# A gated cross-attention and mixture-of-experts layer: attention stacked through DRAM, tokens sorted by expert

## What is computed

```python
x = x + tanh(g_xattn[0]) * xattn(layernorm(x), ctx, ctx, wq, wk, wv)
x = x + tanh(g_ffn[0]) * ffn(layernorm(x), Wr, br, W1, b1, W2, b2)
# xattn: Q, K, V by 16 heads of 8; softmax(Q K^T / sqrt(8)) V
# ffn: D = 128, hidden 256, E = 8, K = 2
logits = jnp.einsum('btd,de->bte', x, Wr) + br
topv, topi = jax.lax.top_k(logits, K)
sel_mask = jax.nn.one_hot(topi, E, dtype=logits.dtype).sum(-2) > 0
gates = jax.nn.softmax(jnp.where(sel_mask, logits, neg_inf), axis=-1)
h = jax.nn.relu(jnp.einsum('btd,edh->bteh', x, W1) + b1)
out = jnp.einsum('bte,bteh,ehd->btd', gates, h, W2)
out = out + jnp.einsum('bte,ed->btd', gates, b2)
```

## Time and profile before

| | us |
|---|---|
| median of 3 runs (816.5 to 819.39) | 818.69 |
| the profiled execution | 816.67 |
| its span, from the first instruction to the last | 814.7 |
| TensorE busy | 731.7 |
| VectorE busy | 586.8 |
| ScalarE busy | 561.7 |
| GpSimd busy | 357.9 |

### The profile page before, as it was taken

The page is one execution under the profiler, slowest core; times in us unless marked ns, Lnnn a source line. Parts: engine busy times, 40 slices in busy tenths (PEclk is TensorE's granted clock), DMA queues, the critical chain, the costliest instruction groups (busy, mean ns, idle before and its releaser), DMA issues. The chain is left out here.

```text
span 814.7 us, 24508 instructions
## 1 busy us (share of the span) xinstructions
PE 731.7 (90%) x7494; PEld 592.9 (73%) x7616; DVE 586.8 (72%) x2271; ACT 561.7 (69%) x1301; POOL 357.9 (44%) x524
## 2 busy tenths in 40 slices
PE   3678999989899998999989999898979999999997
PEld 1455787878678786778868787777867878787765
DVE  3777878777777777777767777577777777778643
ACT  3587777767667675867767687576767767677532
POOL 4555444544444443454444344344444445444400
PEclk9867999999999999999999999799999999999999
DMA  5000000000000000010000001000000000000000
GB/s 174 2 1 23 1 23 14 23 15 22 17 3 23 14 23 16 2 36 2 23 16 23 15 2 36 2 23 15 22 16 2 23 14 23 15 2 15 1 15 13
DMA packets 20583, 15.20 MB, mean 19 GB/s; under 512 B 1552, under 2 KB 20112, under 8 KB 20208
## 3 DMA queue, kind: packets, MB, share of 16 engines
q1 hardware_dynamic: 19632, 13.21, 5.4%
q10 hardware_dynamic: 832, 0.41, 0.2%
HBM read 9.42 MB, written 4.19 MB: 17 GB/s over the span
## 5 line engine op out<-in xcount | busy, mean ns | idle before, releaser
L962 POOL TENSOR_TENSOR probs_lo<-probs 77x512 bf16<-77x512 f32 x256 | 261.5, 1041 | 137.8 <-ACT probs L533 137.6
L449 PE MATMUL y<-w_sb,hidden 128*128 128x128 f32 x2048 | 286.3, 285 | 0.0
L449 PEld LDWEIGHTS y<-w_sb,hidden 128*128 128x128 f32 x2048 | 268.3, 198 | 3.9
L560 ACT ACTIVATE hidden<-hidden_p,b_sb 128x512 f32<-128x512 f32 x256 | 175.5, 686 | 70.2 <-PE hidden_p L431 70.1
L533 ACT ACTIVATE probs<-scores 77x512 f32<-77x512 f32 x256 | 152.2, 595 | 8.3 <-PE scores L373 7.9
L708 DVE TENSOR_REDUCE neg_max<-max_scores 128x4 f32<-128x308 f32 x256 | 120.7, 471 | 34.8 <-PE max_scores L355 34.3
L724 DVE SCALAR_TENSOR_TENSOR acc<-y,gates,acc 128x128 f32<-128x128 f32 x384 | 107.9, 344 | 35.9 <-PE y L449 35.9
L428 PE MATMUL hidden_p<-xT,w_lo 128*128 128x512 bf16 x253 | 100.1, 396 | 20.2 <-issue 12.2
L373 PE MATMUL scores<-qmT,kT 128*77 128x128 bf16 x1024 | 103.8, 226 | 1.8 <-ACT probs L533 1.7
L373 PEld LDWEIGHTS scores<-qmT,kT 128*77 128x77 bf16 x1024 | 85.7, 121 | 26.8 <-issue 5.7
L431 PE MATMUL hidden_p<-xT_mid,w_sb 128*128 128x512 bf16 x256 | 98.7, 385 | 0.6 <-ACT xT_mid L656 0.4
(11 more groups left out here) (102 smaller groups left out, 1178.5 us busy)
## 6 DMA issues: line engine op xcount, KB each, us to landing
x_in<-x SPq DMA_DIRECT2D x16, 256.0 KB, 3.1
out<-result SPq DMA_DIRECT2D x16, 256.0 KB, 2.3
ctx_in<-ctx_t SPq DMA_DIRECT2D x16, 154.0 KB, 3.0
w_sb<-w SPq DMA_DIRECT2D x2, 1024.0 KB, 12.5
b_rows<-b ACTq DMA_DIRECT2D x1, 384.0 KB, 9.9
w_att<-w_att_t SPq DMA_DIRECT2D x1, 192.0 KB, 5.1
gates_in<-g_xattn ACTq DMA_DIRECT2D x1, 0.5 KB, 3.3
gates_in<-g_ffn ACTq DMA_DIRECT2D x1, 0.5 KB, 4.9
```

Source lines behind the costliest of these rows:

```text
L449: last = mm(y_bank[:, cut], hidden[k][:, cut], w2_sb[:, w], start=False, stop=(c == HC - 1), skip_group_check=True)
L560: nc.scalar.activation(hidden[m % 4][:], hidden_bank[m % 2][:], ACT.Relu, bias=b1_sb[:, m:m + 1]).then_inc(s_relu, 1)
L962: G.tensor_tensor(probs_lo[h][:], probs[h][:], upper(probs[h][:]), ALU.subtract).then_inc(s_plo[h], 1)
```

## The change

It is a rewrite. The sequences 0 to 55 are sorted by expert in five chunks of 8, 12, 12, 12 and 12; the sequences 56 to 63 go through all experts as before. The program is a list of 100 slots without loops; a planner at build time gives the slots of routing, scattering, experts, gathering and adding. By its rules the quads stand in slots 37, 39 to 43, 51 to 58, 63 to 70 and 75 to 90, the scattered rows in slots 30 to 33, 42 to 47, 54 to 59, 66 to 71 and 78 to 80, the gathers of the last chunk in 93 to 95, the experts of the last eight sequences in 81 to 96.

Attention: projections are made per four sequences (512 or 308 columns). K and Q, split in high and low bf16 halves, are stored to DRAM and read back so that a head's 8 rows lie interleaved as (high, high, low, ones or maxima) on 32 partitions; the maxima take the same way. The transposes of Q and K on TensorE go. The products with V keep the f32 probabilities and write head j's 9 rows to the strip of 32 partitions j of one bank; ScalarE copies that bank, TensorE turns it with four f32 transposes, VectorE normalises. The probabilities' low halves are no longer made.

Experts: for each chunk VectorE ranks the tokens by expert, and GpSimd scatters each token's row twice to DRAM, to its place among its experts' rows. The rows are read back in quads of four tiles of 128, turned by the transfer itself; 38 quads in all. Each tile belongs to one expert, whose number TensorE loads from SBUF into a register (`name_weights`), and the weights' addresses are made from it. ScalarE stores the outputs from its own queue; GpSimd gathers each token's two outputs; VectorE adds both with their gates. Biases of the hidden layer become a product (`b1_split`). Weights, the cleared rows and constants are moved in pieces from ScalarE's queue.

```diff
-ATT_LAG = 2
-EXPERT_LAG = 7
+CHUNKS = (8, 12, 12, 12, 12)
+DENSE = 8
+MAX_LAG = 8
+SCORE_LAG = 13
+OUT_LAG = 14
+ROUTER_LAG = 20
...
+QUADS = [(2 * n + 8) // 4 for n in CHUNKS]
+ROUTED = [SEQ0[c] + CHUNKS[c] - NB + ROUTER_LAG for c in range(NC)]
+RANKED = [t + 2 for t in ROUTED]
+PLACED = [t + 5 for t in ROUTED]
+SCATTER_AT, QUAD_AT, ADD_AT = [], [], []
+t = 0
+while len(ADD_AT) < SB:
+    late = t >= LAST_ATT
+    for _ in range(4 if late else 2):
+        last = QUAD0[CHUNK_OF[len(ADD_AT)]] + QUADS[CHUNK_OF[len(ADD_AT)]] - 1 if len(ADD_AT) < SB else NQ
+        if len(SCATTER_AT) < SB and PLACED[CHUNK_OF[len(SCATTER_AT)]] < t:
+            SCATTER_AT.append(t)
+        elif len(QUAD_AT) > last and QUAD_AT[last] + 3 <= t:
+            ADD_AT.append(t)
+    if len(QUAD_AT) < NQ and t not in RANKED:
+        c = CHUNK_OF_QUAD[len(QUAD_AT)]
+        whole = SEQ0[c] + CHUNKS[c]
+        if len(SCATTER_AT) >= whole and SCATTER_AT[whole - 1] + (2 if late else 4) <= t:
+            QUAD_AT.append(t)
+    t += 1
+GATED_ALL = B - NB + ROUTER_LAG
+DENSE_AT = [GATED_ALL + 1 + n for n in range(DENSE // NB * E)]
...
-        head = h * PER + j
-        o = o_bank[:, head * VW:(head + 1) * VW]
-        v = v_cols[n % 4][:, head, :]
-        mm(o, hi[:, j * S:(j + 1) * S], v, start=(head == 0), stop=False,
-           skip_group_check=True)
-        last = mm(o, probs_lo[h][:, j * S:(j + 1) * S], v, start=False, stop=True,
-                  skip_group_check=True)
-    last.then_inc(p_pv, 1)
+def values(b, h):
...
+    pe.wait_ge(s_exp, HG * b + h + 1)
+    for j in range(PER):
+        last = mm(oT_bank[ROWS * j:ROWS * j + VW, h * S:(h + 1) * S], v_cols[g % 3][:, b % NB, h * PER + j, :],
+                  probs[h][:, j * S:(j + 1) * S], start=True, stop=True, skip_group_check=True)
+    last.then_inc(p_pv, 1)
+def turn_o(b, t):
+    pe.wait_ge(s_oT, b + 1)
...
+    for h in range(HG):
+        last = nc.tensor.transpose(o_bank[:, h * S:(h + 1) * S], oT[:, h * S:(h + 1) * S], ident[:])
+    last.then_inc(p_oT, 1)
...
+def name_weights(q):
...
+    _, held[q] = nc.values_load_multi_w_load_instructions(
+        tile_w[c % 2][0:1, at_tile:at_tile + 4], engines=[mybir.EngineType.PE], min_val=0,
+        max_val=(E - 1) * HID, skip_runtime_bounds_check_because="DVE clamps the expert's number to 0..7")
+def hidden_part(q, half):
+    k = 2 * q + half
+    if half == 0:
+        pe.wait_ge(s_xs[q % 3], 32 * (q // 3 + 1))
...
+    if k:
+        pe.wait_ge(s_relu, k)
+    w_hi, tiles = upper(w1_sb[:]), xsT[q % 3]
+    for t in range(2 * half, 2 * half + 2):
+        w = held[q][t]
+        cut = slice(t * 128, (t + 1) * 128)
+        for m in range(HC):
+            o = hidden_bank[:, ((t % 2) * HC + m) * 128:((t % 2) * HC + m + 1) * 128]
+            at_w = bass.ds(w + m * 128, 128)
+            mm(o, b1_split[:, at_w], ones_b[:], start=True, stop=False, skip_group_check=True)
+            mm(o, w_hi[:, at_w], tiles[:, 0, cut], start=False, stop=False, skip_group_check=True)
+            mm(o, w1_lo[:, at_w], tiles[:, 0, cut], start=False, stop=False, skip_group_check=True)
+            last = mm(o, w_hi[:, at_w], tiles[:, 1, cut], start=False, stop=True, skip_group_check=True)
+    last.then_inc(p_hid, 1)
+def rows_out(q):
+    pe.wait_ge(s_relu, 2 * q + 2)
...
+    for t in range(4):
+        w = held[q][t]
+        o = y_bank[:, t * 128:(t + 1) * 128]
+        mm(o, ones_b[:], b2_split[:, bass.ds(w, 128)], start=True, stop=False, skip_group_check=True)
+        for m in range(HC):
+            last = mm(o, hidden[:, (2 * q + t // 2) % 4, t % 2, m, :], w2_sb[:, bass.ds(w + m * 128, 128)],
+                      start=False, stop=(m == HC - 1), skip_group_check=True)
+    last.then_inc(p_y, 1)
+def dense_units(n):
...
+    w_hi = upper(w1_sb[:])
+    for m in range(HC):
+        cut = slice(e * HID + m * 128, e * HID + (m + 1) * 128)
+        mm(score_bank[m][:], w_hi[:, cut], dense_rows[g % 2][:, 0, :], start=True, stop=False,
+           skip_group_check=True)
+        mm(score_bank[m][:], w1_lo[:, cut], dense_rows[g % 2][:, 0, :], start=False, stop=False,
+           skip_group_check=True)
+        mm(score_bank[m][:], w_hi[:, cut], dense_rows[g % 2][:, 1, :], start=False, stop=True,
+           skip_group_check=True).then_inc(p_dhid, 1)
+def dense_out(n):
...
+    for i in range(NB):
+        o = to[:, i * D:(i + 1) * D]
+        mm(o, ones_b[:], b2_split[:, e * HID:e * HID + D], start=True, stop=False, skip_group_check=True)
+        for m in range(HC):
+            last = mm(o, dense_hidden[n % 2][:, m, i * S:(i + 1) * S],
+                      w2_sb[:, (e * HC + m) * D:(e * HC + m + 1) * D], start=False, stop=(m == HC - 1),
+                      skip_group_check=True)
+    last.then_inc(p_dy, 1)
...
+def store_k(g):
+    sp.wait_ge(s_klo, g + 1)
...
+    for t, half in ((0, 0), (2, 0), (1, 1)):
+        sp.dma_start(k_dram[g % 2][:, t, :, :].rearrange("p h n -> h p n"), k_hl[g % 2][:, half, :]
+                     ).then_inc(s_kw[g % 2], 16)
+def stack_k(g):
+    sp.wait_ge(s_kw[g % 2], 48 * (g // 2 + 1))
...
+        sp.wait_ge(s_const, 96)
+    planes = k_dram[g % 2].rearrange("p t h (i k) -> (p t) (h i) k", i=NB)
+    for j in range(PER):
+        r = slice(ROWS * j, ROWS * (j + 1))
+        sp.dma_start(k_st[g % 3][r, :, :, j, :], planes[r]).then_inc(s_kst[g % 3], 16)
+def stack_q(g):
+    sp.wait_ge(s_qw[g % 2], 32 * (g // 2 + 1))
...
+    sp.dma_start(q_st[g % 3][:], q_dram[g % 2].rearrange("(h p) t n -> (p t) h n", h=HG)
+                 ).then_inc(s_qst[g % 3], 16)
+def store_max(g):
+    sp.wait_ge(s_nmT, g + 1)
+    sp.dma_start(nm_dram[g % 2], nmT[:]).then_inc(s_nw[g % 2], 16)
+def stack_max(g):
+    sp.wait_ge(s_nw[g % 2], 16 * (g // 2 + 1))
+    sp.dma_start(q_st[g % 3][3::16].rearrange("p h n -> p (h n)"),
+                 nm_dram[g % 2].rearrange("(a b) q -> a (b q)", a=2 * PER)).then_inc(s_nst[g % 3], 16)
+def load_tiles(q):
+    c = CHUNK_OF_QUAD[q]
+    sp.wait_ge(s_scat[c], 32 * CHUNKS[c])
+    if q >= 3:
+        sp.wait_ge(p_hid, 2 * (q - 2))
+    first = 512 * (q - QUAD0[c])
+    for h in range(2):
+        sp.dma_start(xsT[q % 3][:, h, :], xs_dram[c % 2][first:first + 512, h * D:(h + 1) * D],
+                     transpose=True).then_inc(s_xs[q % 3], 16)
...
+def store_y(q):
+    c = CHUNK_OF_QUAD[q]
+    act.wait_ge(s_ys, q + 1)
...
+    first = 512 * (q - QUAD0[c])
+    act.dma_start(ys_dram[c % 2][first:first + 512, :].rearrange(
+        "(t p) w -> p t w", p=128), ys[q % 2][:]).then_inc(s_yst[q % 2], 16)
-    G.tensor_tensor(probs_lo[h][:], probs[h][:], upper(probs[h][:]),
-                    ALU.subtract).then_inc(s_plo[h], 1)
+def scatter(b):
...
+    for k in range(2):
+        G.indirect_dma_start(out=xs_dram[c % 2], out_offset=bass.IndirectOffsetOnAxis(
+            ap=at[k][c % 4][:, i:i + 1], axis=0), in_=rows[c % 2][:, i, :],
+            in_offset=None).then_inc(s_scat[c], 16)
+def gather(b):
...
+    for k in range(2):
+        G.indirect_dma_start(out=back[k][:, b % 16, :], out_offset=None,
+                             in_=ys_dram[c % 2][0:TILES[c] * 128, :],
+                             in_offset=bass.IndirectOffsetOnAxis(ap=at[k][c % 4][:, i:i + 1], axis=0)
+                             ).then_inc(s_back[g], 16)
```

More of the change, by code:

```diff
@@ new lines, in flamingo_kernel @@
+    TILES = [4 * q for q in QUADS]
+    QUAD0 = [sum(QUADS[:c]) for c in range(NC)]
+    NQ = sum(QUADS)
+    NMAX, TMAX = max(CHUNKS), max(TILES)
+    SB, G0 = sum(CHUNKS), sum(CHUNKS) // NB
+    assert SB + DENSE == B and all(n % NB == 0 for n in CHUNKS) and DENSE == 2 * NB
+    CHUNK_OF = [c for c, n in enumerate(CHUNKS + (DENSE,)) for _ in range(n)]
+    SEQ0.append(SB)
+    CHUNK_OF_QUAD = [c for c in range(NC) for _ in range(QUADS[c])]
+    LAST_ATT = B + OUT_LAG
+    ROUTED = [SEQ0[c] + CHUNKS[c] - NB + ROUTER_LAG for c in range(NC)]
@@ L154, in bank @@
+        flat = "p a b -> p (a b)"
+        b1_rows, b1_rest = (back[k][:].rearrange(flat)[0:96, :] for k in range(2))
+        b2_rows, b2_rest = (rows[k][:].rearrange(flat).bitcast(F32)[0:96, 0:E * D] for k in range(2))
         def bank(name):
             return stack.enter_context(nc.psum_tensor(name, [128, 512], F32))
-        score_bank = bank("scores")
         max_bank = bank("max_scores")
-        hidden_bank = [bank("hidden_p0"), bank("hidden_p1")]
-        y_bank = bank("y")
-        o_bank = bank("o")
@@ L245, in group_at, with per @@
-        def group_at(s, n, it, lag):
-            if (n - lag) % NB != 0 or not active(s, lag):
-                return None
-            return group_of(n, it, lag)
+        score_bank = [bank("scores0"), bank("scores1")]
+        oT_bank = bank("bank_oT")
+        o_bank = bank("o")
+        group_bank = bank("group")
+        hidden_bank = bank("hidden_p")
+        y_bank = bank("y")
+        router_out = slice(PER * KEYS, PER * KEYS + NB * E)
+        def per(name, n):
+            return [sem(f"{name}{i}") for i in range(n)]
```

(21 more changed lines are left out.)

1695 lines of the change are left out of this document (910 added, 785 removed).

## The result

The changed kernel takes **717.88 us** (median of 3 runs, 716.36 to 718.5) against 818.69 before: **0.877** of the time, with a 95% interval of 0.8737 to 0.8804. The forecast of 753 was on the right side and 35 us too high. The rest of this document shows that this distance is what is left of larger misses that point both ways.

The account below looks back on a forecast made before the run. TensorE was taken to bound the kernel. Stretches of 48, 163, 373, 10, 28, 85, 7, 31 and 6 us summed to a 751 us span; about 2 us around it gave 753 us, 0.92 of 818.69, range 640 to 875.

Parts of the forecast that it names:

- I take 3.4: Attention's sixteen f32 value products per sequence: 3.4 us at 0.215 each, chosen between bounds of 0.85 and 4.8.
- five steps instead of eight: Strips rival, value products: neighbouring strips overlap, 2.1 us instead of 3.4, 1.25 less per slot, 673 us in all; chance 0.28.
- The switches: Value products: eight switches per slot between strips and full array; draining the engine, they would give back most of strips' gain.
- The loop of a slot: Slot without a quad: 6.3 us of TensorE work plus 0.5 waiting for the first maximum's reduction, 6.8 us.
- The quads: Slot with a quad: 6.8 - 0.5 + 3.9 of quad products + 0.8 of registers, 11.0 us.
- Registers at 0.8 uncovered: Quads: of 36 register instructions (1.3 to 1.5 us) and one register load, 0.8 us per quad stays uncovered.
- The rival of stalled registers: Quads: register addresses stall TensorE, 4.0 us instead of 0.8 per quad, 875 us in all; chance 0.10.
- The maxima's way: Maxima through DRAM: about 7 us against a 6.8 us slot; 1 us charged for some ten groups without quads, 10 us.
- The start: Before slot 13: first maximum at about 24 us, then maxima-only slots and stacking bring slot 13 to 48 us.
- The clock: Rival, slots 13 to 36: granted clock stays at 0.64, 6.3 us become 9.8, 837 us in all; chance 0.10.
- under half-loaded queues 2 us more: Transfers rival, DRAM trips: 2 us more each stalls maxima (+38), slower gathers add 34, 825 us in all; chance 0.10.
- Dense slots: Slots 81 to 90: quad 3.9, dense unit 3.5, registers and waits 1.1, so 8.5 us each, 85 in all.

Follow-up runs that it names:

- experiment 1: The changed kernel with the four value products of a call writing one strip of rows instead of four: 805.12 us, 0.985.
- experiment 4: The changed kernel with three 512-column products standing for all the products of a quad: 649.23 us, 0.795.
- experiment 3: The changed kernel with SyncE issuing the stacked maxima's read ahead of the three k stores, not behind them: 691.11 us, 0.8457.
- experiment 2: The changed kernel with quads addressing weights at constants, not through registers, so most rows pass a wrong expert: 713.43 us, 0.8713.
- Experiments 5 and 8: experiment 3's kernel plus 32-bit, partly later k-stack clears and k-stack reads behind the q store: in all groups (5, 717.57 us) or the first only (8, 689.27 us).

## Why the prediction was right, and where it was not

**The bound.** TensorE's stream sets most of the time in the slots with a quad: experiment 1 put 2.45 us per sequence into it and 1.65 of them showed (9.5 to 11.1); experiment 4 took 3.3 out and 1.7 showed. Without a quad it is less, 1.4 in slots 13 to 36 (6.9 to 8.3). Two waits, for the stacked maxima and for VectorE's maxima through the single bank, take 33.1 + 22.0 = 55 us of the span.

**The value products: the term that failed.** "I take 3.4" was the step, and "lines 306 and 313 are f32 rows whose stationary operand is not the limit" its reason. By starts they measure 4 x 0.34 = 1.4 us per sequence (1.7 as busy time), between the lower bound of 0.85 and the choice. As serial products they measure 4 x 0.97 = 3.9: the pace of lines 306 and 313 was the wrong row, and that of line 449, 0.24 per product, the right one. The rival's "five steps instead of eight" gives 2.1, also too much. The Trainium skill, "TensorE: Matmul & The Clock Gate", Part 3, gives 2.38 times for three strips with products of 512 columns. The trace goes the same way: four strips with f32 products of 128 columns give 2.85. The switches cost little: the 308-column product stands 0.22 us ahead of a value product (131.50 to 131.72) and 0.14 ahead of line 433 (129.03 to 129.17 in the same trace), so entering the strips costs 0.08, four times per sequence, and leaving them is already in the 0.34. The Trainium skill, "TensorEngine Tiling (Array Packing)", Key Properties, has a change of the tiling mode drain the engine. The trace has room for 0.3 us per sequence of that, not for most of the gain, which is what the prediction made of it.

**Why not 673, then.** Experiment 1 splits the 35 us of the miss into two larger ones. With the premise of the forecast the kernel takes 805, 52 more than 753; the strips take 87 off again. In the profiled span of experiment 1, 805.4 against the sum's 751, the 54 us lie in the start (+20), slots 13 to 36 (198.7 for 168, +31) and slots 37 to 76 (392.5 for 378, +14), less 10 in the dense slots and 1 behind them. The rival's 80 us for the strips came near their 87, but it was reached with 1.25 us per slot, where the starts show 2.5, about half of which showed in time. That the forecast's own value premise was wrong and its number only 35 us off is luck of signs.

**The loop of a slot.** 6.8 us was forecast and 6.9 measured in slots 13 to 36, for another reason: not 6.3 of stream plus 0.5, but a shorter stream (135.4 us busy in 24 slots, 5.6 each, at 0.84 of the clock) with waits. Every fourth one ends in the wait for the maxima; with it gone (experiment 3) the mean is 6.2. In experiment 1, where the stream was as long as forecast and 0.5 more, the slots took 8.3: 6.8 us of stream at 0.91 of the clock is an estimate of 7.5, and the busy time was 188.8 / 24 = 7.9.

**The quads.** The 11.1 for 11.0 of experiment 1 is in part luck too: its value products take 0.5 more than was forecast and its registers some 0.7 less. Registers at 0.8 uncovered were wrong; experiment 2 leaves 0.1. The load of four registers, bounded from 0.03 to 3 us, measures 0.33:

```profile
L539 PEldq TENSOR_LOAD <-tile_w x38: 328/333/777, 230.3 to 659.8; - x38
```

The rival of stalled registers falls at the same time.

**The maxima's way.** The mechanism was right and named with its place ("three K stores ... ahead of the read in SP's queue"); its size was not. It was charged at 1 us where no quad stands. The k stores wait for VectorE's half of k, and everything behind them in the queue waits along; experiment 3 puts 27 us on this order, the clock that came back with it included.

**The start.** The first maximum came at 38.8 us, not at 24. Two things were not in the sum: VectorE's clears, three times this row,

```profile
2.17 4.17 DVE L1237 MEMSET k_st<- 128x4928 bf16 x1 [0.98 <-issue]
```

which stand ahead of the statistics and of the halves of k and q, and SyncE's queue, where the store of q stands behind a k stack that waits for its data. As 32-bit words the same clear takes 2.11 us. Experiments 5 and 8 changed both and won 5 of the 15 us. Of the others 8.6 lie in the first two stores, beyond 2.3 us for each, the price that the prediction took for the store of the maxima. So the chain that ended last shows it (start and us):

```profile
16.32 7.95 DMA k_dram<-k_hl
...
29.80 5.27 DMA q_dram<-q_hl
```

No run says why these two took so much longer.

**The clock.** The rival asked for 0.64 before the first quad. The stretch has 0.84, and 0.94 once the maxima's wait is gone. Between these two the same products are busy 10 us less, so an estimate of the whole distance to 1.00 is 16 us of busy time, not 84. "The new products fill over 90% of the slot", the argument against this rival, did not hold: TensorE was busy for 135.4 of 166.0 us, 82%.

**Transfers.** The rows landed later than before (k and q stacks 3.9 us, x 4.9 against the earlier trace rows), but outputs and maxima in 2.5 and 1.7; "under half-loaded queues 2 us more" was half right, and the packets were covered. A gather occupies GpSimd for 0.95 us and stands 1.25 behind the last, for which 1.3 was taken between 0.44 and 3.1. The tail is 42.9 us for 44.

**Dense slots.** 8.5 was forecast and 7.5 measured: TensorE is busy 74.5 of 75.4 us there, so of 1.1 us for registers and waits next to nothing was needed.

**The signs.** Every rival's sign showed: value starts nearer than 0.2 us, gaps with no releaser ahead of lines 560 to 577, a clock under 0.9 before the first quad, waits at line 479. So did two of the forecast's own, 6.9 us between slots for 6.8 and TensorE busy for 88% of slots 13 to 76. A sign said that a mechanism was there; what it cost took an experiment each time.

## What to carry to other kernels

Follow each DMA queue as if it were an engine: one read that the critical engine wants next, behind stores that still wait for their data, cost 27 us here, and moving another read in the same queue lost as much again. Test a sum's terms apart before trusting its total, since two misses of opposite sign look like a hit. Gaps that the profile puts down to issuing are priced by taking the instructions away, not by adding the gaps up.

## What the runs showed of the hardware that was not expected

- f32 products with 128 columns that write to four different 32-row strips of a bank: 0.34 us for four, against 0.97 in the same strip.
- Products whose weight address comes from a register start as close as others when nothing else holds them: 659.66, 659.73, 659.78, 659.84 for lines 560 to 563 in a quad, 0.055 us per 128 columns in the earlier trace rows. Taking away the 36 register instructions of a quad and its load gave back 0.1 us in all.
- One issue of a transposing DMA takes SyncE's queue some 1.25 us (2.64 for two), three times a plain one of the earlier trace rows.
- A read of the k stack's quarter is 0.65 us of issue, against 0.37 for the load of x in the earlier trace rows.
